# Three PSUM banks by turns for the maxima of a 14-wide attention, later transpositions, and small parts moved from VectorE to GpSimd

## What is computed

```python
q, k, v = qkv[0], qkv[1], qkv[2]            # (windows * heads, 196, 16)
attn = einsum('bqc,bkc->bqk', q * scale, k)
rel_h = einsum('bhwc,hkc->bhwk', r_q, Rh)
rel_w = einsum('bhwc,wkc->bhwk', r_q, Rw)
attn = attn + rel_h[..., None] + rel_w[..., None, :]
attn = softmax(attn.reshape(-1, N, N), axis=-1)
out = attn @ v
```

## Time and profile before

| | |
|---|---|
| median of 3 runs | 597.98 us (597.18 to 598.92) |
| the profiled execution | 599.19 us, its span 597.4 us |
| PE busy (matmul) | 524.7 us, 88% |
| PE weight load | 405.3 us, 68% |
| DVE busy | 311.4 us, 52% |
| ACT busy | 222.9 us, 37% |
| POOL (GpSimd) busy | 122.9 us, 21% |
| chain that ended last | PE 61%, DVE 17%, DMA 8%, ACT 6% |
| largest lines of the chain | PE PS L1255 60%, DVE NM L1146 5%, DMA QA<-REL 4%, DMA QA<-NR 3% |

### The profile page before, as it was taken

The page is one execution under the profiler, slowest core; times in us unless marked ns, Lnnn a source line. Parts: engine busy times, 40 slices in busy tenths (PEclk is TensorE's granted clock), DMA queues, the critical chain, the costliest instruction groups (busy, mean ns, idle before and its releaser), DMA issues.

```text
span 597.4 us, 10151 instructions
## 1 busy us (share of the span) xinstructions
PE 524.7 (88%) x3836; PEld 405.3 (68%) x3836; DVE 311.4 (52%) x834; ACT 222.9 (37%) x437; POOL 122.9 (21%) x175
## 2 busy tenths in 40 slices
PE   7987879699989889999798899989878787999997
PEld 5746757588855747467466698857467665888676
DVE  4758776464222723575576644227686863740142
ACT  4314445616343025335232416342145555252210
POOL 5203010142003413134042116020030102320030
PEclk9999688699999989999898999979987796999999
DMA  6882354244314573574456007202804442110001
GB/s 161 209 204 50 70 112 91 78 107 108 90 54 104 117 168 81 115 174 103 117 140 179 1 13 180 57 20 71 188 11 98 86 89 95 38 32 0 1 0 54
DMA packets 22310, 54.74 MB, mean 92 GB/s; under 512 B 5026, under 2 KB 10906, under 8 KB 22166
## 3 DMA queue, kind: packets, MB, share of 16 engines
q1 hardware_dynamic: 22046, 53.99, 37.6%
q10 hardware_dynamic: 216, 0.10, 0.1%
HBM read 11.53 MB, written 0.79 MB: 21 GB/s over the span
## 4 chain that ended last, share of the span: by engine, by line
PE 61%; DVE 17%; DMA 8%; ACT 6%; SPq 4%; issue 3%; DVEq 0%; ACTq 0%
PE PS L1255 60%; DVE NM L1146 5%; DMA QA<-REL 4%; DMA QA<-NR 3%; ACT HT L1013 2%; DVE HL L1159 1%; DMA PT<-in_qm 1%; DVE STAT L1050 1%; DVE OT L1183 1%; SPq L681 1%; DVE HL L1163 1%; DVE OT L1181 1%; DVE REL L1133 1%; PE PS L1372 1%; SPq L682 1%
## 5 line engine op out<-in xcount | busy, mean ns | idle before, releaser
L1146 DVE TENSOR_REDUCE NM<-PS 98x2 f32<-98x392 f32 (+2 forms) x192 | 105.3, 569 | 73.2 <-PE PS L1255 71.5
L987 ACT ACTIVATE PT<-PS 98x392 f32<-98x392 f32 (+2 forms) x192 | 94.1, 521 | 98.6 <-PE PS L1255 94.8
L1255 PE MATMUL PS<-KA,QA 126*98 126x196 f32 (+3 forms) x432 | 97.7, 325 | 22.5 <-DVE NM L1146 16.1
L1255 PE MATMUL PS<-QA,KA 128*98 128x196 f32 (+2 forms) x480 | 95.2, 313 | 10.5 <-DMA QA<-NR 7.4
L1255 PEld LDWEIGHTS PS<-KA,QA 126*98 126x98 f32 (+3 forms) x432 | 65.5, 194 | 47.5 <-DVE NM L1146 30.7
L1255 PEld LDWEIGHTS PS<-QA,KA 128*98 128x98 f32 (+2 forms) x480 | 74.7, 204 | 20.8 <-DMA QA<-NR 9.1
L1255 PE MATMUL PS<-XT,WQKV 96*96 96x512 f32 x128 | 62.7, 622 | 5.1 <-issue 3.9
L1255 PE MATMUL PS<-W,HT 128*128 128x192 f32 x288 | 48.7, 328 | 3.9 <-ACT HT L1013 3.9
L1255 PE MATMUL PS<-PT,V 128*32 128x196 f32 (+2 forms) x672 | 51.4, 352 | 0.0
L1255 PEld LDWEIGHTS PS<-W,HT 128*128 128x128 f32 x288 | 46.6, 190 | 5.9 <-ACT HT L1013 5.9
L1255 PEld LDWEIGHTS PS<-XT,WQKV 96*96 96x96 f32 x128 | 20.5, 171 | 29.3 <-issue 29.3
(11 more groups left out here) (114 smaller groups left out, 698.5 us busy)
## 6 DMA issues: line engine op xcount, KB each, us to landing
QA<-QHL SPq DMA_DIRECT2D x36, 192.0 KB
KA<-KHL SPq DMA_DIRECT2D x24, 228.0 KB
QA<-REL SPq DMA_DIRECT2D x24, 224.0 KB
QA<-QHL SPq DMA_DIRECT2D x12, 384.0 KB
KA<-KHL SPq DMA_DIRECT2D x12, 384.0 KB
KA<-PT SPq DMA_DIRECT2D x12, 380.0 KB
QA<-REL SPq DMA_DIRECT2D x48, 64.0 KB
W1R<-in_w SPq DMA_DIRECT2D x3, 768.0 KB, 4.3
```

What stands on the lines that cost most here:

```text
L987: nc.scalar.activation(dst, src, ACT.Exp).then_inc(probs_done.sem, 1)
L1146: nc.vector.tensor_reduce(dst, src, AX.X, ALU.max, negate=True).then_inc(max_done.sem, 1)
L1255: return nc.tensor.matmul(dst, lhsT, rhs, start=start, stop=stop, skip_group_check=loose)
```

## The change

Four edits, all for the 14-wide layers (`L.pads`):

1. `max_banks` gives `max` and `maxT` the banks 0, 1 and 5 by turns, in the order of the list. Layer 1 keeps its banks.
2. `maxT` of a head comes four maxima behind the head's last one, not two. The last head's `maxT` still follows its last maximum directly.
3. The split of NM into HL is made by GpSimd, in its own order of steps at the last unit of a head; DVE then waits for it before it writes over NM.
4. The second chunk's k split on GpSimd has a step of its own, `later_k`, at score unit (0, 2), behind the split of head 2's maxima.

```diff
-        if j % L.max_units == 1 and j > L.max_units:
+        if j % L.max_units == 3 and j > L.max_units:
             m = j // L.max_units - 1
             out.append(("maxT", m, 0, 0))
             if m == 0:
...
+            if (h, k) == (0, 2):
+                out.append(("later_k", 1, 0, 0))
...
-                if turned < ahead + (taken - 2) // L.max_units:
+                if turned < ahead + (taken - 4) // L.max_units:
                     out.append(("maxT", turned, 0, 0))
                     turned += 1
...
+def max_banks(L):
+
+    banks, turn = {}, 0
+    for step in attention_steps(L):
+        if step[0] == "max" and not L.pads:
+            banks[step[:3]] = MAX_BANK[(L.max_units * step[1] + step[2]) % 2]
+        elif step[0] == "maxT" and not L.pads:
+            banks[step[:3]] = TR_BANK
+        elif step[0] in ("max", "maxT"):
+            banks[step[:3]] = (*MAX_BANK, TR_BANK)[turn % 3]
+            turn += 1
+    return banks
...
-            if step in ("q", "k") and u == 1 and not (L.pads and (step == "q" or i == 0)):
+            if step == "later_k" or step in ("q", "k") and u == 1 and not L.pads:
...
+            elif step == "max" and u == L.max_units - 1 and L.pads:
+
+                if i >= 2:
+                    pool.wait_ge(*maxT_psum.at(n, i - 2))
+                pool.wait_ge(*max_done.at(n, L.max_units * i + u))
+                nm, hl = m["NM"][:, i % 2, :], m["HL"][:, i % 2, :]
+                parts = [(nm[0:HALF_IN, 0:8], hl[0:HALF_IN, 0:8], hl[0:HALF_IN, 8:16]),
+                         (nm[:, 8:10], hl[:, 16:18], hl[:, 18:20])]
+                for full, hi, lo in parts:
+                    ins = nc.gpsimd.tensor_copy(hi, full)
+                ins.then_inc(max_hi.sem, 1)
+                pool.wait_ge(*max_hi.at(n, i))
+                for full, hi, lo in parts:
+                    ins = nc.gpsimd.tensor_tensor(lo, full, hi.bitcast(F32), ALU.subtract)
+                ins.then_inc(max_lo.sem, 1)
...
             elif step == "max":
                 h, p, j = i, i % 2, L.max_units * i + u
+                if L.pads and u == 0 and h >= 2:
+                    dve.wait_ge(*max_lo.at(n, h - 2))
                 dve.wait_ge(*max_psum.at(n, j))
-                bank, nm = MAX_BANK[j % 2], m["NM"][:, p, :]
+                bank, nm = BANKS[n]["max", h, u], m["NM"][:, p, :]
...
-                if u == L.max_units - 1:
+                if u == L.max_units - 1 and not L.pads:
...
-                claim(TR_BANK, maxT_done.at(n, h))
+                bank = BANKS[n]["maxT", h, 0]
+                claim(bank, maxT_done.at(n, h))
```

More of the change, by code:

```diff
@@ L398, in attention_steps @@
     return out
+def max_banks(L):
[9 more added lines that the diff above has]
+    return banks
+BANKS = [max_banks(L) for L in LAYERS]
 def all_steps():
@@ L1153, in _ @@
                     dve.wait_ge(*max_done.at(n, j))
[L1154 to L1160, removed]
+                    hl = m["HL"][:, p, :]
+                    nc.vector.tensor_copy(hl[:, 0:8], nm).then_inc(max_hi.sem, 1)
                     dve.wait_ge(*max_hi.at(n, h))
-                    for full, hi, lo in parts:
-                        ins = nc.vector.tensor_tensor(lo, full, hi.bitcast(F32), ALU.subtract)
-                    ins.then_inc(max_lo.sem, 1)
+                    nc.vector.tensor_tensor(hl[:, 8:16], nm, hl[:, 0:8].bitcast(F32), ALU.subtract)\
+                        .then_inc(max_lo.sem, 1)
             elif step == "maxT":
@@ L1169, in _ @@
                     dve.wait_ge(*max_row_at(L, h - 2))
-                nc.vector.tensor_copy(m["NR"][:, h % 2, :], PS[0:L.max_cols, TR_BANK, 0:L.max_rows])\
+                nc.vector.tensor_copy(m["NR"][:, h % 2, :], PS[0:L.max_cols, BANKS[n]["maxT", h, 0], 0:L.max_rows])\
                     .then_inc(maxT_done.sem, 1)
@@ L1344, in _ @@
                 h, s, j = i, i % L.ring, L.max_units * i + u
-                bank = MAX_BANK[j % 2]
+                bank = BANKS[n]["max", h, u]
                 if u == 0:
@@ L1370, in _ @@
                 pe.wait_ge(*max_lo.at(n, h))
-                claim(TR_BANK, maxT_done.at(n, h))
-                nc.tensor.transpose(PS[0:L.max_cols, TR_BANK, 0:L.max_rows], m["HL"][:, h % 2, :].bitcast(F32),
+                bank = BANKS[n]["maxT", h, 0]
+                claim(bank, maxT_done.at(n, h))
+                nc.tensor.transpose(PS[0:L.max_cols, bank, 0:L.max_rows], m["HL"][:, h % 2, :].bitcast(F32),
                                     IDN[0:L.max_rows, 0:L.max_rows]).then_inc(maxT_psum.sem, 1)
```

## The result

The changed kernel took 605.44 us (median of 10 runs, 600.42 to 608.23), beside 598.64 us for the kernel before on the same chip: a ratio of 1.009, 95% interval 1.0048 to 1.0132. Run a second time, beside other kernels, it took 606.02 us against 600.81: 1.0091 (1.0055 to 1.0126). So it is some 0.9% slower, where 597.4 us, 0.6 less than before, was forecast, and 605.44 lies 3 us above the range. Ratios and intervals leave out the executions that took over 1.5% longer than the fastest of the same kernel, the medians do not, so a ratio can differ a little from that of the medians beside it.

What follows compares the result with a forecast made beforehand. Bound by TensorE's own work (61% of the span), then mostly DVE's reductions, HL work and transfers into QA. Per layer 2.0 + 0.7 - 2.3 - 0.9 + 1.3 - 0.6, rounded to 0.3, gave 597.4 us; range 590.6 to 602.6.

Steps and rivals of the forecast that it cites:

- First maxima: Layer's eighteen first maxima: with three banks most of TensorE's waits for reductions go, 2.0 us saved a layer.
- Head 5: Beside the first inverse on DVE: a later reduction wait and the HL wait go, head 6's scores start 1.3 us earlier.
- Head 9: Second inverse: head 11's transposition waits behind GpSimd's second divide, then 0.75 us of HL; loss 0.6 us (0.3 to 2.3).
- The second k's split: Second chunk: DVE's split of q waits out GpSimd's k subtraction, TensorE's reduction wait grows from 2.7 to 5 us.
- The milder reading: Only the q split's own subtractions wait for GpSimd, not its casts: about 0.8 us lost in place of 2.3.
- the landing of the sixth head: Its transfers into QA, issued behind head 0's later row, delay GpSimd's k split by 0.5 us (0 to 1.2).
- Rows late: Heads without pv: transposition two maxima later shortens the row's cover, scores wait; 0.9 us lost a layer, aug waits gone.
- rival 3: Slower: rows land late, 0.8 us more at heads 3, 4, 7 and 8 of both layers, 603.8 us; chance 0.22.
- Clock: TensorE's two half-clock stretches in layer 0 stay as they are; a stretch more or less is worth half its 3 to 7 us.
- Rival 4: Third bank does nothing, the transposition taking its turn where the waits are: 598 us, inside the forecast's band; no own chance.
- Rival 1: DVE's split of q does not wait for GpSimd: 2.3 us more a layer stay, 592.8 us; chance 0.18.
- Rival 2: Shorter waits of head 5 leave the clock at 2.4 GHz: 3.4 us a layer, 590.6 us; chance 0.15.

Runs made afterwards that it cites:

- E6: The changed kernel with GpSimd's split of the second k waiting until DVE's split of q is done: 600.60 us, ratio 0.9995 to the kernel before.
- E1: The changed kernel with the split of NM into HL on DVE again: 605.01 us, ratio 1.0064 to the kernel before.
- E2: The changed kernel with the transposition two maxima behind again, the sixth head's transfers moving earlier with it: 592.31 us, ratio 0.9837 to the kernel before.
- E3: The kernel before with only the three banks by turns: 593.90 us, ratio 0.9868 to the kernel before.
- E8: The changed kernel with the transposition three maxima behind instead of four: 596.53 us, ratio 0.9921 to the kernel before.
- E7: The changed kernel with the sixth head's transfers ahead of head 0's row in SP's order, as before the change: 605.53 us, ratio 1.0034 to the kernel before.

## Why the prediction was wrong, point by point

**First maxima** (2.0 us a layer): right, 1.9 in layer 2 and in both layers of the second profile. **Head 5** (+1.3): right. From the scores of head 5 to those of head 6 it is 6.2 us for 7.5 in layer 0, and 1.2 are won in layer 2. **Head 9** (-0.6): right, 0.5. GpSimd's divide, then 0.74 us of HL (115.96 to 116.70), for 0.75 forecast:

```profile
114.75 1.26 POOL L900 TENSOR_TENSOR OT<-XNOS,OT 128x512 f32<-128x512 f32 x1 [1.48 <-DVE OT L1213]
115.96 0.32 POOL L890 CAST HL<-NM 98x8 fp32r<-98x8 f32 x2
116.35 0.35 POOL L894 TENSOR_TENSOR HL<-NM,HL 98x8 fp32r<-98x8 f32 x2
116.76 0.38 PE L1403 MATMUL PS<-IDN,HL 120*20 120x120 f32 x1 [3.46 <-POOL HL L894]
```

**The second k's split**: the mechanism was right, and E6 shows it. The wait was put at 5 us and is 4.5. DVE's casts were held by GpSimd's subtraction as assumed (0.82 us alone, 2.56 beside it). With the rule of the Trainium skill, SBUF — State Buffer, section "SBUF: two separate sides", that one of the two holds the port pair for its whole instruction, the trace agrees. The milder reading, that only the split's own subtractions wait, is out. What the hold cost was put too high, 2.3 us a layer for the 1.6 to 1.7 that E6 wins back. What was put too low is the landing of the sixth head, "+0.5 us (0 to +1.2)". Counted from the first maximum it is 1.0 us later in layer 2, and 1.5 in layer 0 of the second profile (in the first profile 3.2, of which 1.6 are the half-clock stretch ahead of it). ACT's copy of the relative rows waited for that landing as well (2.51 us, and 1.59 in layer 2), which I had not seen. At the end of the long wait the forecast is 0.2 us off in layer 2 (the table).

**Rows late** (0.9 us a layer): this is the term of the sum that failed in size. It measured 1.8 us in each layer: from the scores of heads 2, 3, 6 and 7 to those of the next head it took 0.2, 0.5, 0.7 and 0.4 us longer than before (5.03 to 5.25, 4.37 to 4.88, 4.26 to 4.92, 4.52 to 4.91 in layer 0). The sum took 2.3 us from SP to landing at each head, and "0.2 for transfers behind aug data" for all of them. At head 4, whose row is issued right behind another head's aug transfers, it was 2.9:

```profile
74.27 1.39 SPq L774 DMA_DIRECT2D QA<-NR  x2
...
77.25 0.42 PE L1285 MATMUL PS<-QA,KA 128*98 128x196 f32 x2 [1.95 <-DMA QA<-NR]
```

From 74.27 to 77.2; at heads 3, 6, 7 and 8, whose row is issued longer after the last aug transfer, it is 2.5 to the start of the scores (93.72 to 96.19 at head 7). So head 4 came 4.88 and 4.81 us behind head 3 in the two layers and not 4.35: 0.5 a layer. Heads 6 to 9 lost 1.2 us in layer 2 (-0.7 to +0.5 in the table) where 0.6 was forecast: head 6 took 4.92 us as forecast (4.9, in layer 0), but from head 7 to head 8 it was 4.9 and not 4.35, since head 7 ran at 1.2 GHz and I had reckoned it at full clock. That is rival 3, the slower one, and its condition (above 2.3 us while aug is in flight) held, though with 0.6 us at one head a layer and 0.2 at four, not 0.8 at four. Its own time, 603.8, had been left outside the range, whose upper end was 602.6.

**Clock** ("I leave these as they are"): this is the step that failed beside it, a term put at nothing. The reason given was that the idle time ahead of each fall remains. It left out that new idle time brings new falls, of which rival 3 alone spoke. In two of the three profiled executions with this order (the changed kernel's second, and E1) one comes in dense pv. And in all three the half-clock stretch that had 6.7 us around head 5 of layer 0 begins in head 6's row wait and has 10.3 (90.4 to 100.7 in the first profile). By the estimate above the clock is 1 to 3 of the 5.2 us.

Together: the forecast was a gain of 0.6 us, the measurement a loss of 5.2 to 6.8. With the clock's time the same, the layer lost 0.8 us for a gain of 0.3 (layer 2), so 2.2 us of the miss are the terms of the sum, nearly all of it the late rows. The rest, 3.6 us or more, is what layer 0 and the clock add, and only an estimate divides it. That the miss is as small as 1.3% is luck: without the later transposition the change wins 9.6 us (E2), for which the sum had about 2, and the later transposition takes back 13, for which it had about 2 besides the long wait. The two errors nearly cancel.

**Rival 4**, that the third bank does nothing, is out: E3 wins 8 us with it. That is more than the 2.0 us a layer that my sum gives the banks at the first maxima and some 1 us at head 5, and it has 17 us less at 1.2 GHz. **Rival 1** needed the split and GpSimd to miss each other; E6 made them. Its price was 4.6 us, the time fell by 5.4, and the trace shows 3.3 of it at the split. **Rival 2** didn't happen in the changed kernel, where that fall only came later, at head 6.

What I never weighed is the transposition's turn among the banks. I worked out that with four behind, unit u=5 of head 3 depends on the reduction two back, and priced it at 5 us, but didn't ask what another place would do. E2 and E8 show 1.7 and 2.1 us there, for 4.5 with `aug 5` late and 3.3 with it early (E7).

What stays open: how the loss splits between idle time and clock, since part of the half-clock time is idle; why three banks keep the clock up; and what E7's early landing is worth.

## What to carry to other kernels

A chain of small transfers has a length that depends on what is queued ahead of it: price its cover at the worst place, and at the clock which that place has. A new wait ahead of dense matmuls has two prices, its own length and the clock that may fall behind it in only some executions, so a forecast that adds waits should lean to the slow side. Edits that pull both ways are priced each by itself, or two large errors can hide in a small sum. Where buffers go round among several users, a step that is moved also moves which of the others has to wait.

## What the runs showed of the hardware

- Within one kernel, runs differ by 2% without any difference in their work: the kernel before took 596.6 to 609.6 us in one group of 23, and the time goes with the time at 1.2 GHz (correlation 0.92). A single profile can be the fastest of ten.
- The clock fell to 1.2 GHz behind a wait of 1.9 us ahead of dense matmuls in some executions and not in others of the same program.
- DVE's three casts of 96x784 took 0.82 us alone. Begun while GpSimd's subtraction of 96x1216 ran, they took 1.48 (E7), 2.40 (E8) and 2.56 us (changed kernel), and each time ended 0.7 us after that subtraction did (58.36 for 57.66; 56.10 for 55.41; 59.85 for 59.17), as if held until it was over.
- Two SP transfers of a row (QA<-NR) took 2.5 us from the first issue to the start of the matmuls that waited for them, and 2.9 us where they were issued 0.6 us behind another head's three transfers.
- Small instructions cost GpSimd little: its instructions on HL take 0.18 to 0.20 us each. A group of the changed kernel (busy us, mean ns):

```profile
L894 POOL TENSOR_TENSOR HL<-NM,HL 98x8 fp32r<-98x8 f32 x24 | 4.8, 201 | 1.9
```
